# Shorter reciprocal-root chains, an earlier parameter load and regrouped last chains in a convolution-and-FFN block

## The chip, the cores and the metric

The kernel runs on one core of a Trainium2 chip. The metric is the device time of one execution in microseconds (us). The engines of the core are TensorE (PE; its weight loads are listed as PEld), VectorE (DVE), ScalarE (ACT), GpSimd (POOL) and SyncE (SP). SP only starts transfers; ACT and POOL start some too. Each engine has an instruction stream of its own and meets the others through semaphores.

## The reference

`x` is a map of 192 x 192 positions with 128 channels, in float32. Three other maps of that shape (`l_pair`, `protein_pair`, `inter_pair`) are given. What matters here:

```
zn = layernorm(layernorm(x));  pp, lp, ip = layernorm of the three pair maps
ab1, ab2, ab3 = sigmoid(zn @ Wg + bg) * (zn @ W + b) * mask      (64 channels each)
pp, lp, ip    = the same gated projections of the pair maps
block = sum_k pp[i,k] ab1[k,j] + sum_k ab2[i,k] lp[j,k] + ab3 * ip   (per channel)
x = x + sigmoid(zn @ Wend + bend) * (layernorm(block) @ Wsum + bsum) * mask
t = layernorm(x);  two of eight experts are picked for the whole map from the mean of t
y = sum over the two experts of w_e * (gelu(t @ W1e + b1e) @ W2e + b2e)
out = x + layernorm(y + t) * gamma + beta
```

Every layernorm needs, for each position, a mean, a variance and one over the root of (variance + eps). The kernel has no root instruction on the engine that does this; it starts from an integer trick on the bits of the variance and improves the guess by polynomial steps.

## The kernel before

The map is cut into 12 blocks (`NBLK`) of 16 rows. A block is held as 24 tiles (`TPB`) of 128 positions x 128 channels. There are four phases, each an own block of instructions for all engines, with a meeting of the engines between them.

**Projection** (`project_phase`, until about 560 us of the trace). Each block passes over four maps, x in 12 groups of two tiles, the others in 6 groups of four (`GROUPS_A`). For a group, ACT and POOL normalize in place (L551, L590), PE transposes (L641), ACT copies (L562), PE projects (L654), ACT takes the sigmoid (L578), POOL multiplies by the mask in x groups (L611), DVE multiplies (L723 and on). DVE also takes the statistics of tiles (`stats_of`, L672) and runs two chains of small dependent instructions per block (`chain_step`, called "early" and "late") that turn statistics into factor and offset; each step waits on a semaphore for the one before. The tables `STATS_A` and `COEFS_A` say in which group of the pass they are issued; four steps of a chain go into a group. Ahead of the first block `setup_parts` loads 17 parameter arrays (SP takes nine, ACT eight; POOL loads eight more), folds layernorm's weights into the projection weights on PE, and turns the mask.

**Triangle** (`triangle_phase`, until about 717 us) sums the products over k, eight channels at a time, with operands that SP loads from scratch memory.

**Mix** (`mix_phase`, until about 930 us). Per block 12 slots (`PAIRS`) of two tiles. In a slot PE transposes (L1081), makes the gate (L1096) and the 128 channels from 64 (L1101), and every other slot adds eight small products for the router (L1115); ACT and POOL normalize three slots ahead (L1019, L1047); DVE multiplies the two (L1182, `y_c`), takes statistics of x2 (L1165) and of a later block (L1132), and runs one chain per block (`ln_pair_step`) for the block to come: `first, per = (1, 3)` means three steps a slot from slot 1 on. In a slot the first step stands ahead of everything, the second ahead of the product, the third behind the product, ahead of the statistics of x2.

**FFN** (`ffn_phase`, to the end). 72 slots (`SLOTS_D`) of four tiles. In slot S, PE runs the first layer of group S as 12 matmuls of 512 columns (L1555 to L1557), transposes group S + 1 (L1531) and runs the second layer of group S - 1 (L1539). ACT does gelu (L1517) and a copy (L1505). DVE per slot: statistics of group S - 2 (L1632), layernorm of group S + 2 (L1211), the last addition of an older group (`finish`, L1667), the low part of the transposed input (`split_low`, L1625), on which PE's next slot waits, then steps of a layernorm chain (`ln_step`), and the sum with the residual (`add_residual`, L1652). `CHAINS_D` groups the 72 groups into chains, `STEPS_D` says in which slot each step goes, `SCALED_IN` in which slot a group is scaled by ACT (L1500; in the crowded slots two of the four tiles by POOL, L1570, or behind the last slot by DVE, L1658); POOL then multiplies by gamma (L1584), DVE finishes, SP stores pairs of groups. The scaled groups live in a ring of `U_RING` buffers.

Of the kernel before, what the change touches and what calls it, by code (L numbers as in the profile page):

```python
# [18 lines left out]
ALU = mybir.AluOpType  # L19
# [9 lines left out]
NBLK = N // BLOCK_A  # L29
LOW = BLOCK_A  # L30
HIGH = HALF_A
TPB = LOW + HIGH
# [11 lines left out]
CHUNKS = ((0, 8), (8, 16), (16, 24))  # L44
# [41 lines left out]

RSQRT_STEPS = 9
LN_STEPS = 5 + RSQRT_STEPS + 1


def rsqrt_step(v, step, y, t, var):

    if step == 0:
        return v.tensor_scalar(y.bitcast(I32), var.bitcast(I32), -0.5, float(RSQRT_MAGIC), ALU.mult, ALU.add)
    part = (step - 1) % 4
    if part == 0:
        return v.tensor_tensor(t, y, y, ALU.mult)
    if part == 1:
        return v.scalar_tensor_tensor(t, t, 0.375 ** 0.5, var, ALU.mult, ALU.mult)
    if part == 2:  # L100
        return v.scalar_tensor_tensor(t, t, -1.25 / 0.375 ** 0.5, t, ALU.add, ALU.mult)
    return v.scalar_tensor_tensor(y, t, 1.875, y, ALU.add, ALU.mult)
# [65 lines left out]
def setup_parts(nc, d, s, ctx, ps):  # L168
# [32 lines left out]
    n_loads = len(loads)  # L201


    def sync(sp):
        for dst, src in loads[0::2]:
            sp.dma_start(dst, src).then_inc(loaded, 16)

    def scalar(act):
        for dst, src in loads[1::2]:
            act.dma_start(dst, src).then_inc(loaded, 16)  # L210
# [46 lines left out]
    def tensor(pe):  # L257
        pe.wait_ge(ident_made, 2)
        pe.wait_ge(loaded, 16 * n_loads)
        pe.wait_ge(more_loaded, 16 * len(more_loads))  # L260
        ident = s["ident"]
        for bank, cols in ((2, slice(0, P)), (3, slice(P, N)), (4, slice(64, N))):
            m = cols.stop - cols.start
            nc.tensor.transpose(ps[0:m, bank, 0:P], zm_low[:, cols], ident[:])
            nc.tensor.transpose(ps[0:m, bank, P:N], zm_high[:, cols], ident[0:64, 0:64]).then_inc(zm_turned, 1)
        pe.wait_ge(folds_made, 3)
        nc.tensor.matmul(ps[:, 0, :], fold[:], w_raw[:], start=True, stop=False)
        nc.tensor.matmul(ps[:, 0, :], s["ones"][0:1, :], bias_row[:, 0:512], start=False, stop=True).then_inc(folded, 1)
        nc.tensor.matmul(ps[:, 1, 0:CH], foldc[:], ws_raw[0:HID, :], start=True, stop=False)
        nc.tensor.matmul(ps[:, 1, 0:CH], s["ones"][0:1, :], bias_row[:, 512:640], start=False, stop=True).then_inc(folded, 1)  # L270
# [122 lines left out]
def project_phase(nc, d, s):  # L393


    with ExitStack() as ctx:
# [59 lines left out]
        def _(sp):  # L456
# [26 lines left out]

            for k in range(len(CHUNKS)):
                load_third(0, k, 0)
            setup_sync(sp)
            for i in range(1, len(PASSES)):
                for k in range(len(CHUNKS)):
                    load_third(i, k, 0)
# [172 lines left out]
        def _(dve):  # L662
# [72 lines left out]

            for t in range(TPB):
                stats_of(0, 0, t)
            setup_vector_first(dve)
            for step in range(CHAIN_STEPS):
                coef_step(0, LATE, step)  # L740
# [174 lines left out]
PAIRS = TPB // 2  # L915
CHUNK_OF = [k for k, (lo, hi) in enumerate(CHUNKS) for _ in range(lo, hi)]


def mix_phase(nc, d, s):
# [5 lines left out]
    with ExitStack() as ctx:  # L925
# [45 lines left out]
        def next_block(m, par):  # L971
            return (m, 1) if par == 0 else (m + 1, 0)
# [152 lines left out]
        def _(dve):  # L1125
# [43 lines left out]
            def slot(m, par, j):  # L1169
                n = 2 * m + par  # L1170
                now, ahead, behind = there(m, par), there(*next_block(m, par)), there(*last_block(m, par))
                first, per = (6, 7) if isinstance(m, int) and (m, par) == (0, 0) else (1, 3)
                for part in range(max(per, 4)):

                    if (ahead or behind) and j >= first and part < per and per * (j - first) + part < chain_steps:
                        coef_step(*next_block(m, par), per * (j - first) + part)
                    if part == 1 and now:
# [38 lines left out]
def route_parts(nc, d, s, sb, sem, psH, psY):  # L1216
# [173 lines left out]
    def vector_last(dve):  # L1390
# [10 lines left out]
CHAINS_D = [(GROUPS_D * n + lo, GROUPS_D * n + hi) for n in range(NBLK)  # L1401
            for lo, hi in (((0, 6),) if n < NBLK - 2 else ((0, 3), (3, 6)) if n < NBLK - 1 else ((0, 4), (4, 6)))]
CHAIN_D = {G: c for c, (first, end) in enumerate(CHAINS_D) for G in range(first, end)}
CHAIN_SPLIT = 7
STEPS_D = {}
for _c, (_first, _end) in enumerate(CHAINS_D):
    for _step in range(LN_STEPS):
        STEPS_D.setdefault(_end + 1 + (_step >= CHAIN_SPLIT and _end < SLOTS_D), []).append((_c, _step))
CHAIN_SLOT = {c: S for S, steps in STEPS_D.items() for c, _ in steps}
# [3 lines left out]
for _slot in range(SCALE_LAG, SLOTS_D + GROUPS_D):  # L1413
    _room = 1 if _slot < CATCH_UP or (_slot < SLOTS_D and _slot % 2 == 1) else 2
    while _room and _G < SLOTS_D and _slot > CHAIN_SLOT[CHAIN_D[_G]]:
        SCALED_IN.setdefault(_slot, []).append(_G)
        _G, _room = _G + 1, _room - 1
# [3 lines left out]
HALVED_D = SECOND_D | TAIL_D  # L1421
U_RING = 4


def ffn_phase(nc, d, s):

    with ExitStack() as ctx:
# [179 lines left out]
        def _(dve):  # L1607
# [73 lines left out]
            for S in range(LAST_D + 1):  # L1681
# [19 lines left out]
                if 1 <= S < SLOTS_D + 1:  # L1701
                    add_residual(S - 1)
                if S >= SLOTS_D:
                    for G in SCALED_IN.get(S - 1, []):
                        finish(G)
# [67 lines left out]
```

## Time and profile before

| | us |
|---|---|
| three runs | 1456.74, 1457.52, 1469.28 |
| median | 1457.52 |
| the profiled execution | 1466.1 |
| its span, first to last instruction | 1464.2 |
| busy: PE, PEld, DVE, ACT, POOL | 1358.6, 1139.6, 1227.2, 984.7, 1004.4 |
| mean granted TensorE clock, share of full speed | 0.97 |

Rows of the profile name an engine, a line of the kernel, an operation and "out<-in" tiles with sizes. `x3` is the number of instructions merged in a row. In a timeline the first number is the start in us from the beginning of the span, the second the time that the row covers, and in square brackets stands how long the engine had been idle before, and what released it. SPq is SP's queue of transfer starts.

### The profile page before, as it was taken

To read this page: it belongs to the slowest core of one execution; us is meant where nothing else is said; L and a number is where in the kernel's file an instruction comes from. 1 tells how busy PE (TensorE), PEld (TensorE's weight loads), DVE (VectorE), ACT (ScalarE), POOL (GpSimd) and SP (SyncE) were. 2 spreads that over 40 slices of the span, in tenths; PEclk is the share of its full clock that TensorE was granted. 3 is DMA by queue.
4 is the path that set the end of the run, shared out by engine and by line. 5 is a ranking of instruction groups with operands and counts; after the bars stand their busy time and mean duration, and the time that the engine had idled before them with its cause. 6 is when DMAs were issued, how large, how long until landed. Compare 5 with 4: busy or idle time off the path is not lost. (4 is left out here: it accounts for less than half of the span.)

```text
span 1464.2 us, 32189 instructions
## 1 busy us (share of the span) xinstructions
PE 1358.6 (93%) x9880; PEld 1139.6 (78%) x9880; DVE 1227.2 (84%) x4156; ACT 984.7 (67%) x2293; POOL 1004.4 (69%) x1557
## 2 busy tenths in 40 slices
PE   5999999999999996898789999699999999999993
PEld 2877778877788876787666666599999999999983
DVE  6998989999998974666699999677888888888996
ACT  3888888888888883333367777345776766767763
POOL 3999999999999994444378888334555555555563
PEclk9999999999999998999899999699999999999997
DMA  9899999999999999989689996211222222222222
GB/s 214 215 251 250 256 243 242 261 252 253 257 249 232 257 253 253 294 262 289 159 256 297 298 301 203 94 45 56 73 84 67 82 83 77 73 87 73 73 59 71
DMA packets 358395, 270.63 MB, mean 185 GB/s; under 512 B 60721, under 2 KB 333075, under 8 KB 358227
## 3 DMA queue, kind: packets, MB, share of 16 engines
q1 hardware_dynamic: 356528, 267.90, 69.3%
q8 instruction: 82, 1.34, 0.4%
q10 hardware_dynamic: 1426, 0.46, 0.2%
q14 instruction: 87, 0.70, 0.2%
q0 software_dynamic: 272, 0.21, 0.1%
HBM read 174.17 MB, written 94.37 MB: 183 GB/s over the span
## 5 line engine op out<-in xcount | busy, mean ns | idle before, releaser
L1517 ACT ACTIVATE hT<-psH_d,b 128x512 f32<-128x512 f32 x288 | 197.9, 689 | 158.7 <-PE psH_d L1557 158.7
L654 PE MATMUL psZ_a<-w_all,xT_a 128*128 128x128 f32 x1728 | 230.1, 276 | 0.5 <-DVE high_lp L729 0.4
L654 PE MATMUL psZ_a<-w_all,xT_block 128*128 128x384 f32 x576 | 214.3, 495 | 8.1 <-DVE low_ab L723 5.1
L654 PEld LDWEIGHTS psZ_a<-w_all,xT_a 128*128 128x128 f32 x1728 | 209.8, 192 | 3.3 <-ACT xT_a L562 2.4
L578 ACT ACTIVATE sig_a<-psZ_a 128x256 f32<-128x256 f32 (+1 forms) x360 | 153.7, 427 | 80.6 <-PE psZ_a L654 49.3
L590 POOL TENSOR_SCALAR shared<-shared,coefs_early 128x128 f32<-128x128 f32 x468 | 203.4, 450 | 0.0
L641 PE MATMUL psT_a<-ident,shared 128*128 128x128 f32 x1152 | 186.1, 274 | 3.4 <-issue 2.0
L641 PEld LDWEIGHTS psT_a<-ident,shared 128*128 128x128 f32 x1152 | 141.2, 142 | 54.4 <-issue 27.1
L1584 POOL TENSOR_TENSOR u_d<-u_d,gamma 128x512 f32<-128x512 f32 x72 | 96.0, 1334 | 124.5 <-ACT u_d L1500 109.3
L1211 DVE TENSOR_SCALAR shared<-shared,coef 128x128 f32<-128x128 f32 x288 | 179.0, 681 | 1.6 <-POOL xh_b L1591 1.6
L1591 POOL TENSOR_TENSOR xh_b<-shared,b 128x512 f32<-128x512 f32 x72 | 93.2, 1294 | 105.8 <-DVE ffn_sum L1652 104.6
L672 DVE BATCH_NORM_STATS2 stats_early<-shared 128x6 f32<-128x128 f32 x672 | 144.1, 277 | 11.2 <-DMA shared<-in_L_conv_l_pair_dram 6.6
L611 POOL TENSOR_TENSOR sig_a<-sig_a,mask 128x384 f32<-128x384 f32 x144 | 119.4, 829 | 42.4 <-ACT sig_a L578 40.3
L654 PEld LDWEIGHTS psZ_a<-w_all,xT_block 128*128 128x128 f32 x576 | 99.0, 192 | 53.2 <-issue 10.0
L1539 PE MATMUL psY_d<-w,hT 128*128 128x128 f32 x1152 | 134.5, 275 | 0.0
L1539 PE MATMUL psR<-w,hT 128*128 128x128 f32 x1152 | 134.5, 275 | 0.0
L590 POOL TENSOR_SCALAR shared<-shared,coefs_late 128x128 f32<-128x128 f32 x276 | 123.0, 452 | 15.0 <-DVE coefs_late L354 12.2
L1539 PEld LDWEIGHTS psY_d<-w,hT 128*128 128x128 f32 x1152 | 131.6, 192 | 0.1
L1539 PEld LDWEIGHTS psR<-w,hT 128*128 128x128 f32 x1152 | 131.5, 192 | 0.0
L1064 POOL TENSOR_TENSOR x_c<-y_c,shared 128x256 f32<-128x256 f32 x144 | 104.7, 727 | 38.5 <-DVE y_c L1182 36.7
L562 ACT COPY xT_a<-psT_a 128x512 f32<-128x512 f32 x216 | 124.4, 576 | 0.4
L1555 PE MATMUL psH_d<-xT_high,w_high 128*128 128x512 f32 x288 | 120.7, 419 | 4.0 <-issue 3.6
(224 smaller groups left out, 3181.7 us busy)
## 6 DMA issues: line engine op xcount, KB each, us to landing
shared<-in_x_dram SPq DMA_DIRECT2D x48, 512.0 KB, 5.7
scratch_xT<-xT_block SPq DMA_DIRECT2D x36, 512.0 KB, 5.2
shared<-scratch_xT SPq DMA_DIRECT2D x36, 512.0 KB, 5.0
scratch_x<-x_c SPq DMA_DIRECT2D x36, 512.0 KB, 4.1
shared<-scratch_x SPq DMA_DIRECT2D x36, 512.0 KB, 3.6
shared<-in_x_dram SPq DMA_DIRECT2D x48, 256.0 KB, 5.1
shared<-L_conv_protein_pair_dram SPq DMA_DIRECT2D x24, 512.0 KB, 7.3
shared<-in_L_conv_l_pair_dram SPq DMA_DIRECT2D x24, 512.0 KB, 9.2
```

Of the source, the lines that this page charges most:

```text
L562: nc.scalar.copy(turned_x(count, i, t0, size), psT[:, count % 2, 0:size * P]).then_inc(copied, 1)
L578: nc.scalar.activation(sig[:, G % 2, 0:size * k * HID].rearrange("p (t c) -> p t c", t=size), z, ACT.Sigmoid).then_inc(gated, 1)
L590: return nc.gpsimd.tensor_scalar(x, x, r, b, ALU.mult, ALU.add)
L611: nc.gpsimd.tensor_tensor(gates, gates, zm, ALU.mult).then_inc(masked, 1)
L641: ins = nc.tensor.transpose(psT[:, count % 2, j * P:j * P + P], tiles_in[i][:, t0 + j, :], s["ident"][:])
L654: ins = nc.tensor.matmul(out, turned_x(G, i, t0, size)[:, j * P:j * P + P], rhs[i], start=True, stop=True)
L672: ins = v.bn_stats(chain_stats[chain][:, at, :], tiles_in[i][:, t, :])
L1064: nc.gpsimd.tensor_tensor(x2[:, par, 2 * j:2 * j + 2, :], y[:, j % 2], x_in[:, par, 2 * j:2 * j + 2, :], ALU.add).then_inc(x2_made, 1)
L1211: ins = nc.vector.tensor_scalar(s["xh_d"][:, g % 2, i, :], s["x2"][:, t, :], r, b, ALU.mult, ALU.add)
L1517: nc.scalar.activation(hT[:, S % 2, f, :], psH[:, f, :], ACT.Gelu, bias=s["b1"][:, f:f + 1]).then_inc(gelued, 1)
L1539: ins = nc.tensor.matmul(psY[G % 2][:, i * CH:i * CH + CH], hT[:, G % 2, f, i * P:i * P + P], s["w2"][:, f, :], start=(f == 0), stop=(f == ...
L1555: nc.tensor.matmul(psH[:, f, :], high, xT_high[:, G % 2, :], start=True, stop=False)
```

## The change

1. `RSQRT_STEPS` goes from 9 to 8: after the start value, one polynomial step of four instructions becomes one of three (a plain Newton step, `-0.5` and `1.5`); the second keeps its four. `LN_STEPS` goes from 15 to 14, in all chains of all phases.
2. In the setup SP loads six of the 17 parameter arrays and ACT eleven; SP starts them behind two thirds of the first block of x instead of behind all of it. DVE does its part of the folding (`vector_first`) ahead of the statistics of the last third. PE no longer waits for the parameters before it turns the mask.
3. In the mix phase the chain is issued two steps a slot from slot 1 to slot 8 (three in slot 1, one in slot 8), not three a slot from 1 to 6. The first block's own table is as it was, a step shorter.
4. In the FFN the last block's chains cover three and three groups, not four and two. The first of them is issued wholly in slot 70. Behind slot 72 up to three groups are scaled per slot, the ring of scaled groups has eight buffers instead of four, and the finishes are regrouped; the program has one slot fewer.

```diff
-RSQRT_STEPS = 9
+RSQRT_STEPS = 8
...
-    if part == 0:
+    if step in (1, 4):
         return v.tensor_tensor(t, y, y, ALU.mult)
-    if part == 1:
+    if step == 2:
+        return v.scalar_tensor_tensor(t, t, -0.5, var, ALU.mult, ALU.mult)
+    if step == 3:
+        return v.scalar_tensor_tensor(y, t, 1.5, y, ALU.add, ALU.mult)
+    if step == 5:
         return v.scalar_tensor_tensor(t, t, 0.375 ** 0.5, var, ALU.mult, ALU.mult)
...
-        for dst, src in loads[0::2]:
+        for dst, src in loads[0::3]:
...
-        for dst, src in loads[1::2]:
+        for dst, src in loads[1::3] + loads[2::3]:
...
         pe.wait_ge(ident_made, 2)
-        pe.wait_ge(loaded, 16 * n_loads)
...
+        pe.wait_ge(loaded, 16 * n_loads)
         pe.wait_ge(folds_made, 3)
...
-            for k in range(len(CHUNKS)):
+            for k in range(len(CHUNKS) - 1):
                 load_third(0, k, 0)
             setup_sync(sp)
+            load_third(0, len(CHUNKS) - 1, 0)
...
-            for t in range(TPB):
+            for t in range(CHUNKS[1][1]):
                 stats_of(0, 0, t)
             setup_vector_first(dve)
+            for t in range(*CHUNKS[2]):
+                stats_of(0, 0, t)
...
+CHAIN_STEPS_C = LN_STEPS + 2
+STEPS_C = [[] for _ in range(PAIRS)]
+FIRST_STEPS_C = [[] for _ in range(PAIRS)]
+for _step in range(CHAIN_STEPS_C):
+    STEPS_C[1 + max(0, _step - 1) // 2].append(_step)
+    FIRST_STEPS_C[6 + _step // 7].append(_step)
...
-                first, per = (6, 7) if isinstance(m, int) and (m, par) == (0, 0) else (1, 3)
+                steps = FIRST_STEPS_C[j] if (m, par) == (0, 0) else STEPS_C[j]
...
-            for lo, hi in (((0, 6),) if n < NBLK - 2 else ((0, 3), (3, 6)) if n < NBLK - 1 else ((0, 4), (4, 6)))]
+            for lo, hi in (((0, 6),) if n < NBLK - 2 else ((0, 3), (3, 6)))]
...
-        STEPS_D.setdefault(_end + 1 + (_step >= CHAIN_SPLIT and _end < SLOTS_D), []).append((_c, _step))
+        STEPS_D.setdefault(_end + 1 + (_step >= CHAIN_SPLIT and _end < SLOTS_D - 3), []).append((_c, _step))
...
-    _room = 1 if _slot < CATCH_UP or (_slot < SLOTS_D and _slot % 2 == 1) else 2
+    _room = 1 if _slot < CATCH_UP or (_slot < SLOTS_D - 2 and _slot % 2 == 1) else 2 if _slot < SLOTS_D else 3
...
-U_RING = 4
+U_RING = 8
...
-                if S >= SLOTS_D:
-                    for G in SCALED_IN.get(S - 1, []):
+                if S == SLOTS_D + 1:
+                    for G in SCALED_IN[S - 2] + SCALED_IN[S - 1]:
+                        finish(G)
+                if S > SLOTS_D + 1:
+                    for G in ready:
                         finish(G)
```

DVE at the very start, before: 24 tiles' statistics, then the first folding instructions, then the late chain (only its first row is shown).

```order
L672 BN_STATS stats_late<-shared 128x6 x24
L231 TENSOR_TENSOR ln_b_col<-ln_b_col,ln_g_col 128x1
L232 TENSOR_TENSOR lnc_b_col<-lnc_b_col,lnc_g_col 128x1
L233 TENSOR_SCALAR fold<-zeros,ln_b_col 128x128
L234 TENSOR_SCALAR foldc<-zeros,lnc_b_col 64x128
L235 TENSOR_SCALAR bias_row<-bias_row 1x512
L236 TENSOR_SCALAR bias_row<-bias_row 1x128
L339 TENSOR_TENSOR work_a<-stats_late 128x24x2
```

And now:

```order
L676 BN_STATS stats_late<-shared 128x6 x16
L234 TENSOR_TENSOR ln_b_col<-ln_b_col,ln_g_col 128x1
L235 TENSOR_TENSOR lnc_b_col<-lnc_b_col,lnc_g_col 128x1
L236 TENSOR_SCALAR fold<-zeros,ln_b_col 128x128
L237 TENSOR_SCALAR foldc<-zeros,lnc_b_col 64x128
L238 TENSOR_SCALAR bias_row<-bias_row 1x512
L239 TENSOR_SCALAR bias_row<-bias_row 1x128
L676 BN_STATS stats_late<-shared 128x6 x8
L342 TENSOR_TENSOR work_a<-stats_late 128x24x2
```

The folding moved ahead of the last eight tiles' statistics.

DVE in slots 3 and 4 of a block of the mix phase, before (`y_c` is the product that closes a slot's work, `coefs_c` and `work_c` belong to the chain):

```order
L94 TENSOR_SCALAR coefs_c<-work_c 128x48
L1165 BN_STATS stats_c<-x_c 128x6 x2
L1132 BN_STATS stats_c<-tri 128x6 x2
L97 TENSOR_TENSOR work_c<-coefs_c 128x48
L99 SCALAR_TENSOR_TENSOR work_c<-work_c 128x48
L1182 TENSOR_TENSOR y_c<-psW_c,end_gate 128x256
L101 SCALAR_TENSOR_TENSOR work_c<-work_c 128x48
L1165 BN_STATS stats_c<-x_c 128x6 x2
L1132 BN_STATS stats_c<-tri 128x6 x2
L102 SCALAR_TENSOR_TENSOR coefs_c<-work_c,coefs_c 128x48
L97 TENSOR_TENSOR work_c<-coefs_c 128x48
L1182 TENSOR_TENSOR y_c<-psW_c,end_gate 128x256
```

And now:

```order
L1177 BN_STATS stats_c<-x_c 128x6 x2
L1144 BN_STATS stats_c<-tri 128x6 x2
L94 TENSOR_SCALAR coefs_c<-work_c 128x48
L96 TENSOR_TENSOR work_c<-coefs_c 128x48
L1194 TENSOR_TENSOR y_c<-psW_c,end_gate 128x256
L1177 BN_STATS stats_c<-x_c 128x6 x2
L1144 BN_STATS stats_c<-tri 128x6 x2
L98 SCALAR_TENSOR_TENSOR work_c<-work_c 128x48
L100 SCALAR_TENSOR_TENSOR coefs_c<-work_c,coefs_c 128x48
L1194 TENSOR_TENSOR y_c<-psW_c,end_gate 128x256
```

The step between the product and the statistics is gone; the two steps ahead of the product stay.

DVE's last instructions, before, from the statistics of the last group on, without the steps in the middle of the chain:

```order
L1658 TENSOR_SCALAR u_d<-ffn_sum,coef_d 128x128 x4
L116 TENSOR_TENSOR work_d<-stats_d 128x8x2
...
L128 SCALAR_TENSOR_TENSOR coef_d<-work_d,coef_d 128x8
L1658 TENSOR_SCALAR u_d<-ffn_sum,coef_d 128x128 x4
L1667 TENSOR_TENSOR out_buf<-u_d,x_beta 128x512 x2
L1658 TENSOR_SCALAR u_d<-ffn_sum,coef_d 128x128 x4
L1667 TENSOR_TENSOR out_buf<-u_d,x_beta 128x512 x4
```

And now:

```order
L119 TENSOR_TENSOR work_d<-stats_d 128x12x2
...
L131 SCALAR_TENSOR_TENSOR coef_d<-work_d,coef_d 128x12
L1679 TENSOR_TENSOR out_buf<-u_d,x_beta 128x512 x3
L1670 TENSOR_SCALAR u_d<-ffn_sum,coef_d 128x128 x6
L1679 TENSOR_TENSOR out_buf<-u_d,x_beta 128x512 x3
```

Of the twelve scaling instructions and six finishes behind the last matmuls' statistics, six scalings and six finishes are left, and the chain stands first.

## Rows read from the trace of the kernel before

**Rows 1.** Three stretches: us, busy (instructions) by engine, granted clock, DMA share, GB/s.

```profile
80.00:420.00 340.00, 333.22 (x2237) 272.62 (x2236) 310.83 (x1229) 289.27 (x725) 315.84 (x622) 1.00 1.05 250
...
620.00:640.00 20.00, 16.19 (x142) 14.73 (x144) 11.19 (x20) 7.02 (x12) 8.00 (x8) 0.83 0.83 235
...
900.00:1300.00 400.00, 387.60 (x2785) 347.09 (x2784) 328.94 (x819) 254.84 (x490) 215.56 (x189) 0.97 0.25 75
```

**Rows 2.** Timeline of the start, DVE: start us, us covered, what, [idle before].

```profile
12.33 1.65 DVE L672 BATCH_NORM_STATS2 stats_late<-shared 128x6 f32<-128x128 f32 x8 [2.30 <-DMA shared<-in_x_dram]
...
14.12 0.16 DVE L231 TENSOR_TENSOR ln_b_col<-ln_b_col,ln_g_col 128x1 f32<-128x1 f32 x1
...
20.20 0.75 DVE L242 SCALAR_TENSOR_TENSOR w_all<-w_raw,ln_g_col,psZ_a 128x512 f32<-128x512 f32 x1 [1.22 <-PE psZ_a L268]
...
22.64 0.52 DVE L254 COPY mask<-psZ_a 64x96 f32<-64x96 f32 x2
```

**Rows 3.** Waits in the projection phase: us in total, times, longest us.

```profile
PE psZ_a L654 <- ACT xT_block L562: 2.6, 12, 0.2
...
ACT shared L551 <- DVE coefs_early L354: 2.8, 12, 0.2
```

**Rows 4.** Timeline, last two steps of an early chain.

```profile
173.69 0.22 DVE L352 SCALAR_TENSOR_TENSOR coefs_early<-work_a,coefs_early 128x56 f32<-128x56 f32 x1
173.94 0.19 DVE L354 TENSOR_SCALAR coefs_early<-coefs_early 128x56 f32<-128x56 f32 x1
```

**Rows 5.** Timeline of the mix phase, slots of two successive blocks.

```profile
781.67 0.42 DVE L1182 TENSOR_TENSOR y_c<-psW_c,end_gate 128x256 f32<-128x256 f32 x1
...
790.01 0.41 DVE L1182 TENSOR_TENSOR y_c<-psW_c,end_gate 128x256 f32<-128x256 f32 x1
...
790.98 0.41 DVE L1182 TENSOR_TENSOR y_c<-psW_c,end_gate 128x256 f32<-128x256 f32 x1
...
794.68 0.33 PE L1081 MATMUL psT_c<-ident,tri_n 128*128 128x128 f32 x1
...
797.14 0.33 PE L1081 MATMUL psT_c<-ident,tri_n 128*128 128x128 f32 x1
...
797.60 0.41 DVE L1182 TENSOR_TENSOR y_c<-psW_c,end_gate 128x256 f32<-128x256 f32 x1
...
799.18 0.41 DVE L1182 TENSOR_TENSOR y_c<-psW_c,end_gate 128x256 f32<-128x256 f32 x1
...
800.26 0.22 DVE L97 TENSOR_TENSOR work_c<-coefs_c 128x48 f32<-128x48 f32 x1
...
800.63 0.42 DVE L1182 TENSOR_TENSOR y_c<-psW_c,end_gate 128x256 f32<-128x256 f32 x1
```

**Rows 6.** Chain that ended last, in order of time, FFN: start us, us, what.

```profile
1088.05 0.44 PE psT_d L1531 x4
...
1095.12 0.44 PE psT_d L1531 x4
...
1101.89 0.44 PE psT_d L1531 x4
...
1421.30 2.06 issue
```

**Rows 7.** Timeline behind the last matmuls.

```profile
1443.42 2.08 DVE L1658 TENSOR_SCALAR u_d<-ffn_sum,coef_d 128x128 f32<-128x128 f32 x4
...
1444.16 1.26 POOL L1584 TENSOR_TENSOR u_d<-u_d,gamma 128x512 f32<-128x512 f32 x1 [9.88 <-DVE u_d L1658]
...
1445.84 1.12 DVE L120 SCALAR_TENSOR_TENSOR work_d<-work_d 128x8 f32<-128x8 f32 x1
...
1449.21 0.17 DVE L128 SCALAR_TENSOR_TENSOR coef_d<-work_d,coef_d 128x8 f32<-128x8 f32 x1
...
1455.57 3.55 DVE L1667 TENSOR_TENSOR out_buf<-u_d,x_beta 128x512 f32<-128x512 f32 x4
```

**Rows 8.** Timeline of PE in the triangle phase, its longest wait for operands but the first.

```profile
623.81 0.69 PE L846 MATMUL psT_b<-ident,operands_odd 128*128 128x128 f32 x2 [5.06 <-DMA operands_odd<-scratch_lp]
```

More of the change, by code:

```diff
@@ L94, in rsqrt_step @@
         return v.tensor_scalar(y.bitcast(I32), var.bitcast(I32), -0.5, float(RSQRT_MAGIC), ALU.mult, ALU.add)
-    part = (step - 1) % 4
-    if part == 0:
+    if step in (1, 4):
         return v.tensor_tensor(t, y, y, ALU.mult)
-    if part == 1:
+    if step == 2:
[3 more added lines that the diff above has]
+    if step == 5:
         return v.scalar_tensor_tensor(t, t, 0.375 ** 0.5, var, ALU.mult, ALU.mult)
-    if part == 2:
+    if step == 6:
         return v.scalar_tensor_tensor(t, t, -1.25 / 0.375 ** 0.5, t, ALU.add, ALU.mult)
@@ L1171, in slot @@
                 now, ahead, behind = there(m, par), there(*next_block(m, par)), there(*last_block(m, par))
-                first, per = (6, 7) if isinstance(m, int) and (m, par) == (0, 0) else (1, 3)
-                for part in range(max(per, 4)):
-                    if (ahead or behind) and j >= first and part < per and per * (j - first) + part < chain_steps:
-                        coef_step(*next_block(m, par), per * (j - first) + part)
+                steps = FIRST_STEPS_C[j] if (m, par) == (0, 0) else STEPS_C[j]
+                for part in range(max(len(steps), 4)):
+                    if (ahead or behind) and part < len(steps):
+                        coef_step(*next_block(m, par), steps[part])
                     if part == 1 and now:
```

## The prediction, made before the changed kernel ran

> **What bounds the kernel now.** I read the busy time of each engine by stretch first, then who waits for whom in each phase, then the timeline at the places that the diff touches. No single engine bounds the whole. In the projection and in the FFN PE is busy for 98% and 97% of a stretch [rows 1], so DVE work is worth time there only where PE is seen to wait for it. In the mix phase DVE and PE take turns. Ahead of the first matmul, at the phase borders and behind the last matmul nothing covers DVE's chains of dependent steps, and there each microsecond counts in full. So I price the change place by place, each time by the wait that ends last.
>
> **Start.** DVE gets the last third of x at 12.33, takes its statistics until 13.98, and can begin the folding at 14.12, when the parameters are there; it is through with the mask at 23.16 [rows 2], and only then goes on to the pair maps' statistics and the first products. Between 14.12 and 20.20 DVE folds and runs the late chain of 16 steps, and then waits 1.22 for PE [rows 2]: PE's path from the parameters to the folded weights is 6.1, DVE's own work 4.86. With a step at 0.22 (0.25 in a wider chain [rows 4], 0.20 in a narrow one, below) the chain is 3.5 and the folding 1.35. The weights and the mask behind it take 23.16 - 20.20 = 3.0. Now the folding runs while the last third is in flight. With the parameters at P and the last third at T, DVE reaches the end of the mask at max(P + 1.35, T) + 1.65 statistics + 15 steps (3.3) + 3.0, if PE's P + 6.1 doesn't come later. The arrivals in the new order are not in the trace. The last parameter's transfer starts earlier, but POOL's eight loads, which the folding also awaits, are unchanged and hold P back; between T as it was and P as it was I take P = 12.0, with T at most 13.35. That gives 12.0 + 1.35 + 1.65 + 3.3 + 3.0 = 21.3 against 23.2: **1.9** saved. Bounds: P = 14.1 as before gives 23.4, so nothing; an early P with T = 12.3 gives 20.3, so 2.9.
>
> The Trainium skill (DMA: Bandwidth & Descriptors, Issuing engines are not separate DMA queues) says that transfers started by several engines interleave on the same 16 DMA engines, and that this saves only the time to start them. No bytes are removed, so by that page alone the last third comes as much later as the parameters come earlier, and the start gains only the order on DVE; it is the second rival below.
>
> **Projection.** In each of the 12 blocks ACT waits 0.2 for the end of the early chain, and PE waits 0.2 for ACT's copy behind it, 2.6 in all [rows 3]. A step there is 0.25 (173.69 to 173.94) [rows 4]. One step fewer ends the chain 0.25 earlier, which is all of that wait: 12 x 0.22 = **2.6** saved. Bounds 0 (if DVE's next wait takes over) and 2.6. The late chain has no such wait behind it and is priced at nothing; the cover is ACT's and POOL's work on the rest of the map's groups. The transfers move 250 GB/s at a DMA share of 1.05 [rows 1], so they have little left; 0.22 a block asks half a per cent more of them.
>
> **Mix.** A block takes 797.60 - 781.67 = 15.93 [rows 5]. A slot without steps takes DVE 0.97 (790.01 to 790.98), one with three steps 1.45 (799.18 to 800.63), of which the pair ahead of the product takes 0.37 (800.26 to 800.63), the third step thus 0.11. PE needs 2.46 for two slots (794.68 to 797.14), 1.23 a slot. Before, slots 2 to 6 run at DVE's 1.45, and the rest at PE's pace. Now the slots with two steps take 0.97 + 0.37 = 1.34. From the product of slot 1 to that of slot 8: 1.58 (slot 1 to 2, as before), five times 1.34, and 1.17 with one step, 9.45; then five slots at 1.23, 6.15; together 15.60, **0.3** less. It is not the removed step that pays: DVE's own work grows, since the steps kept are the dear ones ahead of the product (six pairs and five thirds, 2.8, become seven pairs, a third and a single, 2.9). What pays is that the slots come nearer to PE's 1.23. Nine blocks have the full pattern (the last two take no statistics of a later block): 2.7. The chain ahead of the first block, the first block's own and the one behind the last block are a step shorter and stand open: 3 x 0.2. Together **3.3**. Bounds: 0.6, and 15.93 - 12 x 1.23 = 1.2 a block would be PE's floor, which the 9.45 excludes; with the waits overlapping at best 0.4 a block, 4.2. The coefficients come at the start of slot 8 and are wanted in slot 9; what is queued behind them on ACT are the copy and the gate of slots 9 and 10.
>
> **FFN, before the tail.** PE's slot is 6.77 (1095.12 to 1101.89), but 7.07 once a block (1088.05 to 1095.12), nine times [rows 6], where DVE comes late with the low part of the input behind eight chain steps. Seven steps now, at 0.22: 9 x 0.2 = **2.0**; in the last blocks PE stands still for 2.06 before slot 70 [rows 6], and once more for less; one step less ahead of each: **0.4**. All 14 steps of the last block's first chain fall into slot 70. They are 2.9 where DVE has no layernorm to do any more; the sum that they delay by about 1 is wanted by PE one slot later, 6.77.
>
> **Tail.** Before, from the end of the last statistics (1443.42): scaling 2.08 for four tiles, the chain from 1445.4 to 1449.38, then 9.7 of scaling and finishing to 1459.12 [rows 7]: 15.7. One step waited 1.12 while POOL multiplied; without that (0.95) a step is 0.20. Now: chain 14 x 0.20 = 2.85, to 1446.3; three finishes, 0.65 each, to 1448.2; six scalings at 0.52, to 1451.3. POOL's products take 1.26 each, the first from 1449.3, so they end at 1450.5, 1451.8 and 1453.1; the last finish ends at 1454.0. That is **5.1** less, and the store behind it is the same. Bounds: 5.8 if DVE scales its first pair while POOL is idle at half the price, 4.3 if DVE's scalings and POOL's products follow one another strictly, as the 1.12 suggests.
>
> The Trainium skill (SBUF — State Buffer, Who interferes with whom) says that such a DVE instruction and a GpSimd instruction hold a shared port pair exclusively, the loser waiting for the whole instruction. The 1.12 beside POOL's 1.26 [rows 7] agrees. By it the tail's saving would be the lower bound, 4.3, and the total 0.8 smaller.
>
> **Sum.** 1.9 + 2.6 + 3.3 + 2.4 + 5.1 = 15.3, against the profiled execution: 1466.1 - 15.3 = 1450.8. That execution is 8.6 above the median of the runs, 1457.52. Nothing in the sum depends on what made it longer, so I carry the saving over: 1442.2, and say 1442.
>
> **Rivals.** (a) *The mix phase gains nothing*: the two steps ahead of the product each expose their full latency and the coefficients come late for ACT in slot 9. For it: DVE's work does grow by 0.1 a block; against it: PE's waiting slots. Saving 12.6, 1444.9. (b) *The start gains only DVE's order*, since the last third of x comes later by what was put ahead of it: saving 0.5 there, 13.9 in all, 1443.6. For it: the page's slices show the DMA engines at eight tenths or more from the start. (c) *The projection is paced by transfers*: at a DMA share of 1.05 the shorter block cannot be fed, and neither it nor the start gains: saving 10.8, 1446.7. Against it: PE's waits there name ACT and DVE. (d) *Slower*: triangle operands. PE there waited 5.06 once [rows 8], and the clock was 0.83 over those 20 us [rows 1], 3.4 more: 8.5 for one such event. The projection is 4.5 shorter, so loads and stores may meet differently. It decides from the second event more than the runs before had: two more cancel the saving (17 against 15.3), three make 1467.7. (e) *The longer ring and regrouped chains do nothing*, because POOL's products pace the tail: saving 10.2, 1447.3; against it, POOL was idle for 9.88 before its first product [rows 7].
>
> **How the numbers follow.** My forecast, all terms within their bounds: 0.56, its own range 1438 to 1446. (a) 0.12, (b) 0.12, (c) 0.10, (d) 0.05, (e) 0.05. A change of 1% is 14.6, about what a measurement of this kernel can tell from no change, so faster by over 1% needs 1442.9 or less: some four fifths of the forecast case and a third of (b): 0.49. Slower by over 1% needs three events of (d): 0.03. The rest, 0.48, is within 1%. The range takes the upper bounds of the start, the mix and the tail (1.0 + 0.9 + 0.7 more), and 3 for the scatter of runs and for stalls of PE that vanish whole, which makes 1436, and up to one event of (d), 1450.6, with (c) inside: 1436 to 1451.
>
> **What would show it.** Start: the mask copies end at 21.3, DVE's wait for the parameters at about 12. Projection: the waits of PE for ACT's copy and of ACT for the early chain are gone, blocks are 43.8 apart. Mix: products 1.34 apart in slots 2 to 7, 15.6 a block. FFN: one slot in six no longer 7.07 but 6.85. Tail: from the end of the last statistics to the last finish 10.6 instead of 15.7. It is wrong if a block of the mix phase is not shorter than 15.9, if the copies of the mask end after 22.5, or if a new wait of ACT for the mix chain stands in every block.

## The result, and the profile of the changed kernel

| | before | changed |
|---|---|---|
| median of 20 runs | 1460.91 | 1452.39 |
| lowest to highest | 1455.86 to 1469.28 | 1447.23 to 1456.76 |
| the profiled execution | 1466.1 | 1447.55 |
| its span | 1464.2 | 1445.6 |
| a second profiled execution, its span | 1461.9 | 1452.8 |

The ratio of the two is 0.9932, with an interval of 0.9917 to 0.9948: 8.5 us less, within 1% of before. I had said 15.3 less, against a median of three runs that stood 3.4 lower than that of the twenty. The spans of the first two profiles are 18.6 apart: the profiled execution of before took 5.2 more than the median of its runs, that of the changed kernel 4.8 less. With two profiles of each kernel averaged the distance is 13.9. So I compare phases, not spans.

The borders in the next table are starts of instructions: PE's first transpose of x, its first one in the triangle phase, DVE's first statistics of tri, PE's first transpose of the FFN phase, and DVE's last statistics (the first of the last four); the tail ends with the end of the last finish. "Block" is the mean distance between the first products of blocks 2 to 9 of the mix phase.

| profile | start | projection | triangle | mix | block | FFN | tail | behind it |
|---|---|---|---|---|---|---|---|---|
| before | 21.54 | 544.72 | 151.22 | 220.37 | 15.93 | 504.79 | 16.48 | 5.08 |
| before, second profile | 21.53 | 543.81 | 152.05 | 218.43 | 15.92 | 504.45 | 16.49 | 5.14 |
| changed | 19.17 | 540.01 | 148.13 | 220.31 | 16.24 | 501.24 | 11.95 | 4.79 |
| changed, second profile | 19.19 | 542.97 | 150.59 | 222.54 | 16.25 | 500.78 | 11.94 | 4.79 |

Of the mean difference of 13.9, the start has 2.4, the projection 2.8, the triangle phase 2.3, the FFN phase 3.6 and the tail with its store 4.9; the mix phase gives back 2.0. Nothing was changed in the triangle phase: over all thirteen profiles of this study it takes 146.75 to 155.43, whichever kernel it is, so its 2.3 is scatter. That leaves 11.6, inside the interval of the ratio (7.6 to 12.1), but 3.1 above the 8.5 of the medians; no run says where these 3.1 are.

The start, DVE's timeline (start us, us covered, what, idle before), answers to [rows 2].

```profile
11.76 0.16 DVE L234 TENSOR_TENSOR ln_b_col<-ln_b_col,ln_g_col 128x1 f32<-128x1 f32 x1 [1.80 <-DMA ws_raw<-in_L_conv_Wsum_dram]
...
13.24 1.65 DVE L676 BATCH_NORM_STATS2 stats_late<-shared 128x6 f32<-128x128 f32 x8
...
18.13 0.74 DVE L245 SCALAR_TENSOR_TENSOR w_all<-w_raw,ln_g_col,psZ_a 128x512 f32<-128x512 f32 x1
...
20.27 0.51 DVE L257 COPY mask<-psZ_a 64x96 f32<-64x96 f32 x2
```

The parameters are there at 11.76 instead of 14.12, the statistics of the last third follow the folding without idle time, and the mask ends at 20.78 instead of 23.16.

Waits of PE in the projection of the changed kernel (us in total, times, longest), the answer to [rows 3]:

```profile
PE psZ_a L658 <- DVE low_ab L727: 5.4, 15, 0.4
PE psT_a L645 <- issue: 2.0, 12, 0.2
```

The wait for ACT's copy of xT_block is gone, and so is ACT's for the early chain. In undisturbed blocks the early chains are 43.79 apart, against 44.05.

Waits in the mix phase from its second block on:

```profile
ACT tri_n L1031 <- DVE coefs_c L1171: 13.2, 10, 1.3
```

This is the new wait that I had named as a sign against the forecast: once in a block ACT stands 1.3 for the coefficients. By itself it costs little: the fastest kernel below, m2, still has it ten times, 5.8 in all.

### The profile page after: what moved, and what is told of

Same layout as the page of the kernel before. It is cut to its first block and busy times, and to the rows that moved or that the text cites. A ratio compares the mean times of both kernels' runs of the same rounds, so it can differ in the third digit from the quotient of the medians.

```text
span 1445.6 us, 32131 instructions
## 1 busy us (share of the span) xinstructions
PE 1351.6 (93%) x9880; PEld 1134.5 (78%) x9880; DVE 1221.8 (85%) x4099; ACT 981.9 (68%) x2295; POOL 1000.4 (69%) x1559
## 3 DMA queue, kind: packets, MB, share of 16 engines
q8 instruction: 82, 1.34, 0.4%
```

## The experiments

### The mix phase: three kernels that place the steps otherwise

The changed kernel has two steps a slot, both ahead of the product. m1 puts back three a slot:

```diff
-    STEPS_C[1 + max(0, _step - 1) // 2].append(_step)
+    STEPS_C[1 + _step // 3].append(_step)
```

> The changed kernel with one line put back: the mix phase's chain (now 16 steps) again three steps a slot. Theory A (the profile of the changed kernel: a slot with two steps, both ahead of the product, takes 1.445, as one with three took before, because the pair ahead costs 0.46 instead of 0.37 and the third step, behind the product, had cost only 0.11; the chain now fills two slots more): slots 2 to 5 at 1.45, one single step in slot 6, a block 15.7 to 15.9 instead of 16.24, ACT's wait for the mask's coefficients gone, time 4 to 5 us below the changed kernel's median (about 1448). Theory B (the two-a-slot table is not at fault; the block grew by the new order of the reciprocal square root's steps): a block stays at 16.2 and the time at 1452.

m2 keeps two a slot, and moves the second behind the product; m3, with (2, 3) in place of (0, 2), moves both behind it, the first ahead of the statistics of x_c, the second ahead of those of tri:

```diff
+                spread = (0, 2) if len(steps) == 2 else tuple(range(len(steps)))
                 for part in range(max(len(steps), 4)):
-                    if (ahead or behind) and part < len(steps):
-                        coef_step(*next_block(m, par), steps[part])
+                    if (ahead or behind) and part in spread:
+                        coef_step(*next_block(m, par), steps[spread.index(part)])
```

> The changed kernel with the second of the two steps of a slot moved behind the product (steps ahead of and behind it, still two a slot). Theory A: a slot is 0.97 + 0.24 (a single step ahead, as in the slot of the mask step, 1.21) + 0.11 = 1.32 instead of 1.445; six of them make a block 0.75 shorter, 15.5, and the time about 7 us below the changed kernel's. Theory C (slots with steps take 1.445 whatever stands in them, since a loop through POOL, PE and ACT paces them, which is why three steps and two give the same): 1.445 again, a block 16.2, time unchanged.

> The changed kernel with both steps of a slot behind the product, one ahead of the statistics of x_c and one ahead of those of tri. Theory A: 0.97 + 2 x 0.11 = 1.19 of DVE, under PE's 1.23, so PE sets the pace in slots 2 to 7: a block 15.0, about 1.2 less than now, and the time 11 to 12 us below the changed kernel's, about 1441. Theory C: a block 16.2, time unchanged.

| kernel | steps a slot | slot | block | median | ratio to before |
|---|---|---|---|---|---|
| before | 3: two ahead, one behind | 1.45 | 15.93 | | |
| changed | 2: two ahead | 1.445 | 16.24 | 1452.39 | 0.9932 (0.9917 to 0.9948) |
| m1 | 3: two ahead, one behind | 1.45 | 15.79 | 1447.83 | 0.9903 (0.9874 to 0.9932) |
| m2 | 2: one ahead, one behind | 1.21 | 14.77 | 1439.75 | 0.9847 (0.9820 to 0.9875) |
| m3 | 2: both behind | 1.46 | 16.13 | 1447.64 | 0.9903 (0.9875 to 0.9931) |

m1 came out as theory A said. m2 gained nearly twice what A gave it (12 instead of 7), and m3, which A had as the best, gained 0.1 a block (its last full block, 14.76 instead of 16.57, and the scatter make the rest; its interval overlaps that of the changed kernel). So A falls: a step has no price of its own that adds up. C, a loop that gives 1.45 whatever stands in a slot, falls by m2. The rows below, DVE and POOL of the same slots, show what sets a slot's length. Before:

```profile
783.26 0.41 DVE L1182 TENSOR_TENSOR y_c<-psW_c,end_gate 128x256 f32<-128x256 f32 x1
...
784.33 0.21 DVE L97 TENSOR_TENSOR work_c<-coefs_c 128x48 f32<-128x48 f32 x1
784.58 0.21 DVE L99 SCALAR_TENSOR_TENSOR work_c<-work_c 128x48 f32<-128x48 f32 x1
784.71 0.42 DVE L1182 TENSOR_TENSOR y_c<-psW_c,end_gate 128x256 f32<-128x256 f32 x1
...
783.75 0.72 POOL L1064 TENSOR_TENSOR x_c<-y_c,shared 128x256 f32<-128x256 f32 x1 [0.45 <-DVE y_c L1182]
```

The changed kernel:

```profile
773.15 0.41 DVE L1194 TENSOR_TENSOR y_c<-psW_c,end_gate 128x256 f32<-128x256 f32 x1
773.48 0.47 DVE L1177 BATCH_NORM_STATS2 stats_c<-x_c 128x6 f32<-128x128 f32 x2
773.88 0.33 DVE L1144 BATCH_NORM_STATS2 stats_c<-tri 128x6 f32<-128x64 f32 x2
774.13 0.30 DVE L98 SCALAR_TENSOR_TENSOR work_c<-work_c 128x48 f32<-128x48 f32 x1
774.47 0.21 DVE L100 SCALAR_TENSOR_TENSOR coefs_c<-work_c,coefs_c 128x48 f32<-128x48 f32 x1
774.59 0.42 DVE L1194 TENSOR_TENSOR y_c<-psW_c,end_gate 128x256 f32<-128x256 f32 x1
...
773.64 0.72 POOL L1076 TENSOR_TENSOR x_c<-y_c,shared 128x256 f32<-128x256 f32 x1 [0.32 <-DVE y_c L1194]
```

m3:

```profile
775.88 0.40 DVE L1195 TENSOR_TENSOR y_c<-psW_c,end_gate 128x256 f32<-128x256 f32 x1
...
776.71 0.44 DVE L100 SCALAR_TENSOR_TENSOR coefs_c<-work_c,coefs_c 128x48 f32<-128x48 f32 x1
777.08 0.34 DVE L1144 BATCH_NORM_STATS2 stats_c<-tri 128x6 f32<-128x64 f32 x2
777.34 0.40 DVE L1195 TENSOR_TENSOR y_c<-psW_c,end_gate 128x256 f32<-128x256 f32 x1
...
776.37 0.73 POOL L1076 TENSOR_TENSOR x_c<-y_c,shared 128x256 f32<-128x256 f32 x1 [0.36 <-DVE y_c L1195]
```

m2:

```profile
771.40 0.41 DVE L1195 TENSOR_TENSOR y_c<-psW_c,end_gate 128x256 f32<-128x256 f32 x1
771.73 0.19 DVE L96 TENSOR_TENSOR work_c<-coefs_c 128x48 f32<-128x48 f32 x1
...
772.49 0.19 DVE L98 SCALAR_TENSOR_TENSOR work_c<-work_c 128x48 f32<-128x48 f32 x1
772.61 0.41 DVE L1195 TENSOR_TENSOR y_c<-psW_c,end_gate 128x256 f32<-128x256 f32 x1
...
771.89 0.73 POOL L1076 TENSOR_TENSOR x_c<-y_c,shared 128x256 f32<-128x256 f32 x1
```

POOL begins its addition x_c 0.49 behind the start of the product and is at it for 0.72. The DVE step that stands there ends 0.05 to 0.07 behind the end of x_c every time: 784.54 against 784.47, 774.43 against 774.36, 777.15 against 777.10, 772.68 against 772.62. In two of the four it was stretched to end there. In the changed kernel it starts 0.98 behind the product and takes 0.30, in m3 it starts at 0.83 and takes 0.44; where nothing holds such a step it takes 0.19 (c4, below). The trace books the difference as work. DVE does not show an idle moment. The statistics and the product between the same products are not held.

So there is a loop: product, 0.49, POOL's addition 0.72, end of the held step 0.07, and whatever DVE has to do between that step and the next product. In the changed kernel this is the second step (0.04 to its start, 0.13 to the product): 0.49 + 0.72 + 0.07 + 0.17 = 1.45. In m3 the held step stands ahead of the statistics of tri: 0.49 + 0.73 - 0.02 + 0.26 = 1.46.

In these slots of before, m1 and m2 no step is stretched. There a step behind the product pushes the next one to 1.07 or 1.10 behind the product, where with its own 0.19 to 0.21 it ends just as x_c has ended. In before and m1 DVE's own work fills the slot: 1.10, then 0.35 for the pair, 1.45. Taking the third step out let the pair start 0.11 sooner, and the hold took the 0.11 back. So beside an addition of 0.72 the third step costs nothing, but the reason is that two limits, DVE's own work and the loop, happen to be equally long. In m2 one step stands ahead of the product, which starts 0.11 behind that step's start: 1.10 + 0.11 = 1.21, nothing held. That is below PE's 1.23 [rows 5], and 14.77 is 12 x 1.23. PE is busy for the whole of five blocks, 73.80 (in the changed kernel for 78.10 of 81.21), so PE sets the pace; the row is m2's, columns as in [rows 1]:

```profile
767.30:841.10 73.80, 73.80 (x662) 53.56 (x661) 71.58 (x390) 54.73 (x181) 66.15 (x121) 1.00 1.05 321
```

The Trainium skill (SBUF — State Buffer, Who interferes with whom) says that a DVE instruction with both inputs in SBUF, or in one of its fast modes, and a GpSimd instruction that reads SBUF take the shared port pair in turns, each for its whole length. The rows agree: the steps (both inputs in SBUF) are held, until 774.43 and 777.15 against the 774.36 and 777.10 of x_c; the product (one input in PSUM, 0.41) and the statistics (one input, 0.47 and 0.33) are not.

### POOL's addition halved

That x_c holds the step was so far read from coinciding times. c4 shortens the suspected cause in the changed kernel; it leaves out the addition for half of the channels, so its output is not the block's:

```diff
-                nc.gpsimd.tensor_tensor(x2[:, par, 2 * j:2 * j + 2, :], y[:, j % 2], x_in[:, par, 2 * j:2 * j + 2, :],
-                                        ALU.add).then_inc(x2_made, 1)
+                half = slice(0, CH // 2)
+                nc.gpsimd.tensor_tensor(x2[:, par, 2 * j:2 * j + 2, half], y[:, j % 2, :, half],
+                                        x_in[:, par, 2 * j:2 * j + 2, half], ALU.add).then_inc(x2_made, 1)
```

> The changed kernel with POOL's addition x_c made for half of the channels only (128x2x64 instead of 128x2x128; the other half is left zero by one fill ahead of the phase, so that half of the addition is left out), about 0.37 instead of 0.72. Theory D (a DVE step with two SBUF inputs, or a fast one, waits until POOL's addition has ended: in each of the runs the step ends 0.07 behind x_c, and product, 0.49 to x_c, 0.72, step, pair close a loop of 1.445): the first step ahead of the product takes 0.20 instead of 0.30, and the slots with two steps take DVE's own 0.97 + 0.37 = 1.34 or PE's pace, a block 15.2 to 15.5. Theory A (the pair ahead costs 0.46 by itself): the slots stay at 1.445 and the block at 16.2.

One execution, 1436.8 us, span 1434.9. The addition takes 0.46, and the slot of the same steps is:

```profile
772.13 0.41 DVE L1196 TENSOR_TENSOR y_c<-psW_c,end_gate 128x256 f32<-128x256 f32 x1
...
773.11 0.19 DVE L98 SCALAR_TENSOR_TENSOR work_c<-work_c 128x48 f32<-128x48 f32 x1
773.33 0.21 DVE L100 SCALAR_TENSOR_TENSOR coefs_c<-work_c,coefs_c 128x48 f32<-128x48 f32 x1
773.46 0.41 DVE L1196 TENSOR_TENSOR y_c<-psW_c,end_gate 128x256 f32<-128x256 f32 x1
...
772.62 0.46 POOL L1077 TENSOR_TENSOR x_c<-y_c,shared 128x128 f32<-128x128 f32 x1 [0.47 <-DVE y_c L1196]
```

x_c now ends at 773.08, ahead of the step at 773.11, and the step takes 0.19. The slots are 1.33, which is the 1.34 of the prediction. DVE's instructions are the same as in the changed kernel; only POOL's is shorter. That shows the cause (theory D). The block, 15.06, is shorter than the 15.2 expected, because slots without such a pair gained too: the first one of a block fell from 1.64 to 1.50, the last from 1.44 to 1.18.

### Each part alone

c1 has the start of the change alone, c2 the chains and ring of the last block, c3 the shorter root with the mix phase's old table, d2 the mix phase's new table with the root of nine steps.

> The kernel before with the start part of the change alone (parameters in front of the last third of x, spread over two queues, the folding ahead of the last third's statistics). Theory: the mask copies end 2.4 earlier, as in the changed kernel (20.8 instead of 23.2), every other phase is as before (projection blocks 44.05, mix block 15.93, FFN 7.05 once in six, tail 16.5 from the last statistics to the last finish), so 2.4 of the median, ratio 0.9984. Rival: the last third comes later and the first projection block gives the gain back: the first triangle transpose as far behind the first projection transpose as before plus 2.

> The kernel before with the tail part alone (chains of three and three groups, ring of eight, finishes grouped; 15 steps a chain as before). Theory: the last statistics to the last finish take 12.2 instead of 16.5 (the 11.95 of the changed kernel and one step of 0.2), the store behind it 0.3 less, and the stall ahead of slot 70 no longer pulls the clock down, 1.5: together 6, ratio 0.996. Rival: the tail gains only with the shorter chain: 14.5 or more.

> The kernel before with the shorter reciprocal square root alone (8 steps instead of 9, mix phase still three steps a slot). Theory: projection blocks 43.8 (2.4 to 2.9 over the phase), mix block 15.77 (nine times 0.16, 1.5), FFN's long slot 6.83 instead of 7.05 (nine times 0.22, 2.0), together 6 to 6.5, ratio 0.9957. Rival: the new order of steps costs as much in the mix phase as the projection gains: mix block 16.2.

> The kernel before with the mix phase's table of the change alone (two steps a slot, both ahead of the product; 17 steps, as the reciprocal square root has its 9). Theory D (a slot with steps takes 1.445 with two steps as with three, set by the product, POOL's addition and the pair ahead; so the chain only lasts longer, now until slot 8): a block 16.5 against 15.93, times ten 5.5, less about 1 in the first block and at the border, ratio 1.003. The prediction's reading (two steps make a slot of 1.34): a block of 15.7 to 15.8 and ratio 0.998.

| kernel | start | projection | mix | block | FFN | tail | median | ratio to before |
|---|---|---|---|---|---|---|---|---|
| c1 | 19.17 | 547.26 | 219.01 | 15.93 | 501.99 | 16.48 | 1459.55 | 0.9983 (0.9960 to 1.0005) |
| c2 | 21.27 | 544.07 | 220.29 | 15.93 | 504.84 | 12.16 | 1459.18 | 0.9981 (0.9963 to 0.9998) |
| c3 | 21.28 | 542.62 | 215.69 | 15.78 | 500.16 | 16.28 | 1452.10 | 0.9937 (0.9916 to 0.9958) |
| d2 | 21.56 | 548.10 | 223.12 | 16.37 | 502.05 | 16.49 | 1464.56 | 1.0027 (1.0007 to 1.0047) |

The four ratios multiply to 0.9928, against 0.9932 measured for all together, so the parts do not work on each other beyond what the runs can tell. c1's start repeats the 2.4, though its ratio is not clear of 1. Its projection is 2.5 longer than that of before, which looks like the rival; but d2, which leaves the start alone, has 548.10. The early chains of c1 stand 44.03 to 44.10 apart in six of eleven blocks and up to 45.30 in the others, and one of these has a wait of 0.95 of PE for the product ip_prod. PE's waits for ip_prod sum to 2.2 in c1 and 2.8 in d2, and to 0.2 in before. Why DVE is late in such single blocks is open; they come in kernels of both kinds. DVE waits for transfers in this phase for 24.9 in c1, the most of all profiles (before 10.9 and 15.0, changed 13.1 and 20.1, d2 15.3), so that the new order of loads makes some later transfers late is not excluded. c2 has 4.3 of tail and 0.3 of store, as expected, but not the 1.5 of the clock (below). c3 is the largest part by far, about 9, above the 6 to 6.5 expected, with the expected ratio just inside its interval. d2 shows the new table as a loss by itself: 16.37 a block where 15.7 to 15.8 would have followed from a slot of 1.34.

### One more gain that moved on

d1 adds to m2 another sharing of the early chain, so that its dear first steps lie further apart:

```diff
-share_out(COEFS_A, AT_X + 4, 4, EARLY, 0, range(CHAIN_STEPS))
+share_out(COEFS_A, AT_X + 4, 3, EARLY, 0, range(3))
+share_out(COEFS_A, AT_X + 5, 4, EARLY, 0, range(3, 7))
+share_out(COEFS_A, AT_X + 6, 5, EARLY, 0, range(7, 12))
+share_out(COEFS_A, AT_X + 7, 4, EARLY, 0, range(12, CHAIN_STEPS))
```

> The kernel with one step ahead of and one behind the product (m2), and beside it the projection's early chain shared out 3, 4, 5, 4 steps over its four groups instead of 4, 4, 4, 4: the first group holds the dear steps (0.93, 0.31, 0.22 and three instructions of together 0.73), and PE waits 0.39 there once in every block. Theory E: that wait goes, a projection block 43.45 instead of 43.80, about 3 to 4 us off m2's 1439.75, ratio to before 0.982. Theory F (the same work has to be through by the same product one group later, so the wait only moves to that product): a block 43.7 to 43.8 and no change of time. Theory of the mix phase in both: block 14.77 again.

Median 1436.38, ratio 0.9834 (0.9808 to 0.9859). The blocks are 43.75, 0.04 less than with m2. PE waits once in a block for the product low_ab. PE's timeline in d1, and the step of the chain that stands ahead of this product, with POOL's multiplication by the mask beside it:

```profile
82.53 1.53 PE L661 MATMUL psZ_a<-w_all,xT_block 128*128 128x384 f32 x4 [0.39 <-DVE low_ab L730]
...
81.19 0.72 DVE L104 SCALAR_TENSOR_TENSOR work_a<-work_a 128x56 f32<-128x56 f32 x1
...
81.02 0.83 POOL L618 TENSOR_TENSOR sig_a<-sig_a,mask 128x384 f32<-128x384 f32 x1 [0.20 <-ACT sig_a L585]
```

The same step and multiplication in the changed kernel, where PE's wait of 0.39 ends at 79.65:

```profile
78.30 0.74 DVE L348 SCALAR_TENSOR_TENSOR work_a<-work_a 128x56 f32<-128x56 f32 x1
...
78.13 0.83 POOL L615 TENSOR_TENSOR sig_a<-sig_a,mask 128x384 f32<-128x384 f32 x1 [0.23 <-ACT sig_a L582]
```

The wait is as long as it was, two groups later, where theory F had it one later. These rows fit a hold as well: other steps of this chain take 0.22, this one 0.72 and 0.74, and it ends 0.06 and 0.08 behind POOL's multiplication (81.91 against 81.85, 79.04 against 78.96). In d1 another step of the chain is the stretched one, and PE's wait went with it. No run shortened POOL's instruction here, so this is read from coinciding times alone. The 3.4 between the medians is not shown by the phases (projection 542.02 against 541.88), and the intervals of m2 and d1 overlap. What is settled is that both are faster than the changed kernel: m2 by 0.85% of the time before.

### The scatter

> The kernel before, unchanged, profiled once more, for the scatter of one kernel's phases. Theory S (the scatter sits in the triangle phase and in single blocks of the projection): mix block 15.93, FFN slot 7.05 once in six, tail the same to 0.1 us as in the first profile; the triangle phase, 151.2 there, off by some us, and the two projection blocks of 44.74 not there or elsewhere. Rival: all phases differ a little, as a changed clock would make them.

> The changed kernel, unchanged, profiled once more. Theory S (start, mix, FFN and tail repeat to 0.1 or 0.2 us, and what differs sits in the projection's single long blocks and in the triangle phase): start 19.2, mix block 16.24, tail 11.95 again; projection 540 to 542, triangle 146 to 153, and a span 2 to 8 above the 1445.6 of the first profile. Rival: another phase moves by over 1.

The second profiles are in the table of phases: 1463.6 us for before and 1454.74 for the changed kernel. Start, mix blocks and tail repeat to 0.02 us, the FFN phase to 0.5. The projection moves by 3.0, the triangle phase by 2.5, and so, against theory S, do the mix phase's first block and its border to the FFN phase (2.2 together).

## Why the prediction was right, and where it was not

The direction held, and relative to before the range did: 0.9932 of the 1457.52 that I had started from is 1449.0, inside 1436 to 1451. The time itself, 1452.39, is 1.4 above that range, since before takes 3.4 more in twenty runs than in three. The size was 15.3 forecast against 8.5 measured (interval of the ratio: 7.6 to 12.1); one of five terms had the wrong sign and left its own bounds (0.6 to 4.2). That the range held all the same is in part luck: it was wide because of an event in the triangle phase, 8.5, that did not come, and the miss of the mix phase used up that room.

**Start**: 1.9 forecast, 2.4 measured. P was 11.76 instead of 12.0, the weights and the mask behind 18.13 took 2.65 instead of 3.0, and the last third was not late: its statistics waited for nothing at 13.24. Rival (b) falls.

**Projection**: 2.6 forecast. Blocks 43.8 apart as promised, 12 x 0.26 = 3.1, and 2.8 between the averaged phases. Both waits went, as the prediction's step had it. Rival (c), pacing by transfers, falls: the undisturbed blocks are shorter by what the chain is.

**Mix**: 3.3 gained forecast, 2.0 lost measured. Of the 6.8 that the sum was too high this is 5.3; by the phases the other terms gave 1.6 more than forecast, and the 3.1 named above are open. The step that failed is "Now the slots with two steps take 0.97 + 0.37 = 1.34". Its reading of the slot of 1.45 [rows 5] as a sum of DVE's own instructions was right for before; the error was to carry the 0.37 of the pair to another place in the slot. The pair (800.26 to 800.63 before) now begins 0.11 sooner, since the third step is gone, runs into POOL's addition, of which the prediction had no row, and takes 0.46, which is the same end. So slots stayed at 1.445, and the chain fills more of them: from the third product of a block on the distances were 1.45 three times, 1.42, 0.98, 0.97, and are 1.445 four times, 1.56, 1.21. From the second product to the ninth that makes 10.13, where I had 9.45, and nearly all of this stays in the block (16.24 against 15.60). Block by block the loss is larger than the 2.0: ten blocks are 0.28 to 0.65 longer, 3.8 in all, and the first block and the border, which scatter by 2.2, gave 1.8 back. c4 shows that 1.34 is right once POOL's addition is short. Rival (a) named the place and the sign (no gain, coefficients late for ACT) but not the cause or a loss.

**FFN**: 2.0 forecast for the slot once a block, measured 7.05 to 6.84, 9 x 0.21 = 1.9. For the stall ahead of slot 70 I had 0.4. The stall itself fell from 2.06 [rows 6] to 1.84. But behind it the granted clock differed (columns as in [rows 1]); the first row is of before, 2.06 of stall ahead of it:

```profile
1423.40:1428.00 4.60, 4.60 (x14) 3.63 (x15) 3.00 (x7) 2.09 (x4) 2.96 (x2) 0.63 0.49 151
```

the second of the changed kernel, with 1.84:

```profile
1411.20:1415.80 4.60, 4.60 (x29) 4.04 (x30) 3.42 (x8) 3.66 (x7) 2.98 (x2) 1.00 0.50 153
```

and the third of c1, with 2.06:

```profile
1417.90:1422.50 4.60, 4.60 (x29) 4.04 (x30) 3.42 (x8) 3.66 (x7) 2.98 (x2) 1.00 0.48 148
```

With the stall at 2.06 or 2.07 the distance from the last but one group to the last was 10.64 to 10.66 in three profiles of five (before twice, c2) and 9.07 to 9.08 in two (c1, d2); with 1.82 to 1.84 it was 8.83 to 8.86 in all eight. The clock of the 4.6 us behind the stall is 0.63 in the first three and 1.00 in the other ten. So the term is 0.2 that is certain and 1.6 that came in some executions, and the sizing missed the second. How often the 1.6 came in the twenty runs of each kernel is not known, and that the shorter stall keeps the clock up is an inference from thirteen profiles.

**Tail**: 5.1 forecast. DVE's timeline of the changed kernel:

```profile
1429.77 0.20 DVE L119 TENSOR_TENSOR work_d<-stats_d 128x24 f32<-128x24 f32 x1
...
1432.48 0.17 DVE L131 SCALAR_TENSOR_TENSOR coef_d<-work_d,coef_d 128x12 f32<-128x12 f32 x1
1432.57 1.89 DVE L1679 TENSOR_TENSOR out_buf<-u_d,x_beta 128x512 f32<-128x512 f32 x3
1434.37 3.58 DVE L1670 TENSOR_SCALAR u_d<-ffn_sum,coef_d 128x128 f32<-128x128 f32 x6
1437.87 2.95 DVE L1679 TENSOR_TENSOR out_buf<-u_d,x_beta 128x512 f32<-128x512 f32 x3
```

Chain 2.88 (forecast 2.85), three finishes 1.89 (1.95), six scalings 3.58 where I had 6 x 0.52 = 3.1, and the last finish ends at 1440.82: 11.1 behind the end of the last statistics, where before had 15.6 by the same measure, so 4.5 (16.48 to 11.95 in the table), and 0.3 at the store. The part that was mis-sized is the scalings beside POOL's products. The 5.1 of the sum left out that DVE's scalings and POOL's products hold each other up; the measured 4.5 lies nearer to the bound of 4.3 that supposed it. Rival (e) falls: c2 has the tail's gain by itself. Of rival (d) nothing shows: PE waited for operands in the triangle phase for 22.5 and 21.0 in the two profiles of before, and for 20.2 and 21.8 in those of the changed kernel.

**The base**: three runs gave 1457.52, twenty gave 1460.91. The level did not carry over, and of the saving 8.5 of 15.3 did.

## What to carry to other kernels

A slot's length is the sum of an engine's instructions only if none of them is stretched. Before pricing a removed step by "slot with it less slot without", look at the same instruction's duration in both kinds of slot, and at what the other engines end at that moment. Here a small DVE step added nothing, about 0.1, or over 0.2 to a slot, by its place relative to POOL's addition, and moving one step behind the product gave 1.5 us a block and 12 us in all (0.9847 against 0.9932), more than any of the change's parts.

Where a kernel's profiled executions scatter by 1%, compare phases over two profiles of each kernel before you explain a difference of spans.

## What the runs showed of the hardware

A DVE instruction held back by POOL is booked as busy for the time that it is held (0.30 and 0.44 us instead of 0.19), with no idle time and no releaser, so neither the list of waits nor the chain of waits tells of it. PE's stall of 2.06 or 2.07 us was followed by a granted clock of 0.63 over 4.6 us in some executions and by 1.00 in others of kernels that are the same at that place, worth 1.6 us. 0.63 as a mean of a stretch says that about three quarters of it ran at the lower level, 1.2 GHz.
